# Channel mix of a two-layer sequence model: two halves of 128 channels summed on GpSimd ahead of one averaging product, and another order of squares and scaling

## The reference

```python
def _layernorm(x, g, b):
    m = jnp.mean(x, axis=-1, keepdims=True)
    v = jnp.mean(jnp.square(x - m), axis=-1, keepdims=True)
    return (x - m) * jax.lax.rsqrt(v + LN_EPS) * g + b
...
xp = jnp.concatenate([x[:, -1:], x[:, :-1]], axis=1)
xn = _layernorm(x, g2, b2)
kk = xn @ W_cm                                  # 256 -> 1024
kk = kk * cmk4 + xp4 * (1.0 - cmk4)
rr = jax.nn.sigmoid(xn * cmr + xp * (1.0 - cmr))
vv = jnp.square(jax.nn.relu(kk)) @ W_cp         # 1024 -> 256
x = x + rr * vv
```

## Time and profile before

| | us |
|---|---|
| median of 3 timed runs | 2118.95 (2117.96 to 2119.46) |
| the profiled execution's own time | 2109.22 |
| span of the profiled execution | 2107.5 |
| channel mix, from the block's start to the next stage's first product | some 1205 to 1436 |
| PE busy over the span | 1907.0 (90%) |
| DVE busy | 1357.6 (64%) |
| ACT busy | 963.3 (46%) |
| POOL busy | 247.8 (12%) |

### The profile page before, as it was taken

One profiled execution on the slowest core, in us unless ns is written; L12 is line 12 of the kernel. 1 busy time (PEld: TensorE's weight loads), 2 busy tenths in 40 slices (PEclk: granted clock), 3 DMA queues, 4 the chain that ended last, 5 costly groups with the idle time before them and its releaser, 6 DMA issues. The chain is left out here.

```text
span 2107.5 us, 31872 instructions
## 1 busy us (share of the span) xinstructions
PE 1907.0 (90%) x11154; PEld 1617.0 (77%) x11154; DVE 1357.6 (64%) x2810; ACT 963.3 (46%) x1801; POOL 247.8 (12%) x229
## 2 busy tenths in 40 slices
PE   8999999983999999996777589998999999999999
PEld 5788888872899999994445357776888888888887
DVE  7567788774666666665999878884444445345342
ACT  4656666643444444435888555542323232232221
POOL 0000012334233232331000000000000000000000
PEclk9999999995999999998888789999999999999999
DMA  3299411323544332233223413413000000000000
GB/s 105 72 364 408 149 49 59 113 84 106 144 106 88 81 85 47 41 46 110 70 60 90 97 44 120 160 51 139 1 21 20 0 20 9 11 20 0 20 11 11
DMA packets 86146, 170.32 MB, mean 81 GB/s; under 512 B 7264, under 2 KB 49888, under 8 KB 85856
## 3 DMA queue, kind: packets, MB, share of 16 engines
q1 hardware_dynamic: 65968, 132.47, 18.0%
q0 software_dynamic: 18176, 33.70, 8.1%
q10 hardware_dynamic: 1888, 2.67, 0.4%
HBM read 91.61 MB, written 88.74 MB: 86 GB/s over the span
## 5 line engine op out<-in xcount | busy, mean ns | idle before, releaser
L2690 ACT ACTIVATE x_tok<-bank,scl 128x512 f32<-128x512 f32 x128 | 88.3, 690 | 360.2 <-PE bank L2741 359.4
L2740 PE MATMUL bank<-hAh,ffn_h 128*128 128x512 f32 x512 | 202.7, 396 | 0.7 <-DVE x_tok L2617 0.7
L2740 PE MATMUL bank<-hBh,ffn_h 128*128 128x512 f32 x512 | 201.7, 394 | 0.0
L2741 PE MATMUL bank<-hAl,ffn_h 128*128 128x512 f32 x512 | 199.4, 389 | 0.0
L2741 PE MATMUL bank<-hBl,ffn_h 128*128 128x512 f32 x512 | 199.3, 389 | 0.0
L1487 POOL DMA_INDIRECT tokens_behind_spare_rows<-yg,row_of_token x70 | 129.5, 1850 | 302.7 <-DVE row_of_token L1655 283.1
L1590 ACT ACTIVATE h<-bank,b1s 128x256 f32<-128x256 f32 x280 | 124.8, 472 | 31.9 <-PE bank L1415 19.8
L2598 DVE CAST hBh<-x_tok 128x1024 fp32r<-128x1024 f32 x48 | 33.3, 693 | 157.6 <-ACT x_tok L2690 157.0
L2598 DVE CAST hAh<-x_tok 128x1024 fp32r<-128x1024 f32 x48 | 33.3, 693 | 148.7 <-ACT x_tok L2690 148.2
L911 ACT ACTIVATE L<-bank 128x512 f32<-128x512 f32 x128 | 75.4, 595 | 106.1 <-PE bank L1169 105.9
L1177 PE MATMUL bank<-st,L 128*128 128x128 f32 x768 | 116.3, 278 | 6.3 <-DVE st L549 6.2
(11 more groups left out here) (447 smaller groups left out, 5498.6 us busy)
## 6 DMA issues: line engine op xcount, KB each, us to landing
z_by_expert<-zero SPq DMA_DIRECT2D x64, 520.0 KB, 16.0
ckb<-in_ffn_dram POOLq DMA_DIRECT2D x32, 352.0 KB, 3.5
xg<-z_by_expert SPq DMA_DIRECT2D x36, 260.0 KB, 3.3
x_tok<-in_w_dram SPq DMA_DIRECT2D x8, 1024.0 KB, 7.7
ffn_h<-ffn_copy SPq DMA_DIRECT2D x2, 4096.0 KB, 14.9
x_tok<-after_time_mix SPq DMA_DIRECT2D x15, 512.0 KB, 7.5
st<-in_w_dram SPq DMA_DIRECT2D x6, 1024.0 KB, 7.3
x_tok<-x_T SPq DMA_DIRECT2D x9, 512.0 KB, 4.2
```

The source lines that it names most:

```text
L2690: A_.activation(gq[:, m % 4, :], B[2 + m % 4][:, :], ACT.Gelu, scale=scl[:, off[nm] + m:off[nm] + m + 1]).then_inc(g_act, 1)
L2740: T.matmul(out, w, x[0], start=first, stop=False)
L2741: return T.matmul(out, w, x[1], start=False, stop=last)
```

## The change

On POOL, a new section adds the two halves: `hm` = half 0 + half 1 of the block ahead of its mean, and `hv` = the same of the squares. PE then runs one product of `avg` with the sum, in place of two. `hm` lies in the place of `rs`, so POOL's sum for block b waits until scale(b-1) has read `rs` (`xs_rdy`), until mean(b-1) has read `hm` (`mean_ps`), and for the block's load. `hv` waits for the squares and for variance(b-1). On ACT, squares(b+1) now comes ahead of parts(b+1), which moves behind deviation(b+1). On DVE, scale(b+1) moves from behind low(b, 1) to ahead of square_keys(b, 2).

```diff
+        hm, hv = rs, in_x_tok(1536, BT)
+        hm_rdy, hv_rdy = sem("mean_halves_summed"), sem("square_halves_summed")
...
+        @block.gpsimd
+        def _(pool):
+            P = nc.gpsimd
+
+            def sum_mean(b):
+                pool.wait_ge(cin_ld[b % 2], loaded(b))
+                pool.wait_ge(xs_rdy, b)
+                pool.wait_ge(mean_ps, b)
+                P.tensor_tensor(hm[:, :], IN[:, b % 2, 0, 0, :], IN[:, b % 2, 0, 1, :], ALU.add).then_inc(hm_rdy, 1)
+
+            def sum_squares(b):
+                pool.wait_ge(sqr_rdy, b + 1)
+                pool.wait_ge(var_ps, b)
+                P.tensor_tensor(hv[:, :], sq[:, 0, :], sq[:, 1, :], ALU.add).then_inc(hv_rdy, 1)
+
+            for b in range(1, NB + 1):
+                sum_mean(b)
+                sum_squares(b)
...
                     keys(b, i)
                     if i == PAIRS - 1 and nxt:
                         low_x(b + 1)
+                    if i == PAIRS - 2:
+                        scale(b + 1)
                     square_keys(b, i)
                     low(b, i - 1)
-                    if i == PAIRS - 2:
-                        scale(b + 1)
...
                 high(b, 0)
-                if nxt:
-                    parts(b + 1)
                 squares(b + 1)
                 high(b, 1)
                 deviation(b + 1)
+                if nxt:
+                    parts(b + 1)
                 high(b, 2)
...
             def mean(b):
-                pe.wait_ge(cin_ld[b % 2], loaded(b))
-                for k in range(KT):
-                    last = nc.tensor.matmul(B[0][:, :], avg[:, :], IN[:, b % 2, 0, k, :], start=(k == 0), stop=(k == KT - 1))
-                last.then_inc(mean_ps, 1)
+                pe.wait_ge(hm_rdy, b)
+                nc.tensor.matmul(B[0][:, :], avg[:, :], hm[:, :], start=True, stop=True).then_inc(mean_ps, 1)
 
             def variance(b):
-                pe.wait_ge(sqr_rdy, b + 1)
-                for k in range(KT):
-                    last = nc.tensor.matmul(B[1][:, :], avg[:, :], sq[:, k, :], start=(k == 0), stop=(k == KT - 1))
-                last.then_inc(var_ps, 1)
+                pe.wait_ge(hv_rdy, b)
+                nc.tensor.matmul(B[1][:, :], avg[:, :], hv[:, :], start=True, stop=True).then_inc(var_ps, 1)
```

## The result

The changed kernel takes 2109.22 us, median of 6 runs (2107.51 to 2113.44), against 2118.45 (2116.54 to 2119.46). The ratio is 0.9960, with a 95% interval of 0.9947 to 0.9972: faster by some 8.5 us, between 6 and 11 (the two medians differ by 9.2). The forecast was 2112.3.

A forecast was written before the change was run, and what follows sets the result against it. A 26.3 us loop through DVE's values, PE's products and variance, then DVE and ACT, not the mean, bounds the kernel. Iterations 0 to 7 sum to -6.65 us: median 2118.95 becomes 2112.3; range -4 to -9.5 us.

The forecast's parts named there:

- The loop runs past the mean: In iterations 2 to 7 the 0.86 us saved on the mean buys nothing, since PE still waits for DVE's values.
- The variance saves 0.86: On PE the variance lies on the loop; one product fewer saves 0.86 us per iteration if hv is in time.
- POOL first by 0.18 us, the square held to 2.2 us: POOL's sum of squares starts 0.18 us ahead of DVE's square_keys(b, 1), which then takes 2.2 in place of 1.22 us.
- The order gives 0.07, the hold costs 0.2: Scale's new place on DVE gains 0.07 us; POOL's hold of square_keys delays Exp, so scale waits 0.2 us.
- Steady iterations -0.7 each: Iterations 2, 3, 4, 6 and 7: 0.86 + 0.07 - 0.2, about 0.7 us saved each, together -3.5.
- Iteration 5, a late mean for 0.85: A late load makes POOL's sum and the mean late, costing 0.85 us against 0.7 gained: +0.15.
- rival (3): Bubbles of 1 us at the mean bring PE's clock down, 2.5 us in each of six iterations: 2127; chance 5%.
- Iteration 0: Squares move forward and the variance starts 0.9 us earlier, at PE's low clock: -1.5 us, bounds 0.8 and 2.8.
- Iteration 1: No values to wait for, so mean and variance both count, 1.71 us, and 0.07 for the order: -1.8.
- Rival 1: DVE's square_keys starts ahead of POOL, so hv comes 1.2 us late: 2119.8, no change; chance 0.26.
- Rival 2: POOL gets no turn between DVE instructions that follow each other; PE stands 2.4 us: 2128.2; chance 0.16.
- rival 4: A float32 product of a sum on PE takes as long as two, so nothing is saved: 2121; chance 3%.

The follow-up runs named there:

- mean alone: The changed kernel with the variance back to two products and both old orders, only the mean's halves summed on POOL; ratio 1.0000 to the unchanged kernel.
- after: The kernel with the full change, against the unchanged kernel; 2109.22 us, ratio 0.9960.
- orders alone: Only the two new orders on ACT and DVE, no POOL sums, two products each; ratio 0.9981 to the unchanged kernel.
- parts ahead: The changed kernel with ACT's old order, parts back ahead of squares; ratio 1.0033 to the unchanged kernel.
- POOL second: The changed kernel, but POOL's sum of squares also waits until DVE has ended square_keys(b, 1); ratio 1.0051 to the unchanged kernel.

## Why the prediction was right, point by point

- *The loop runs past the mean.* Right. The mean alone gave a ratio of 1.000, and PE's 0.85 us of new waiting equals what was saved. A count of passes (32 fewer at 0.43 us, 13.7 us) would have promised twice the gain. The passes did fall by 32, and PE's busy time in the stage by 12.0 us (211.7 to 199.6), for 6.85 us of time. I had looked for some 13 us in PE's busy time over the whole execution, and there it fell by 7.3 only (1907.0 to 1899.7), as other stages, in which no line differs, moved by some us the other way.
- *The variance saves 0.86.* The step was right; the size is 0.95: from its start to the second half of keys(b, 2) it is 3.82 us against 4.72, and the 36 products before it took 0.05 less.
- *POOL's sum, 1.29 us.* It is 1.26 to 1.30 where nothing holds it.
- *POOL first by 0.18 us, the square held to 2.2 us.* Right to the hundredth, because both starts hang on the same DVE run: POOL's by way of centre and squares, the square's by way of centre and keys.
- *The Trainium skill's rule* (SBUF — State Buffer, Who interferes with whom) holds here for two SBUF inputs, which rows 9 could not show: the square and low are held for the rest of POOL's instruction, and POOL for the rest of theirs. Keys, with one SBUF input and one in PSUM, kept their 0.75 us beside POOL's sum.
- *The order gives 0.07, the hold costs 0.2.* The first was mis-sized: it is 0.31, with a hold of 0.25. The net on the way to L was put at a loss of 0.13 and came out as a gain of 0.06. Parts' cover held: high(b, 2) starts 0.03 us behind the end of the square that it needs.
- *Steady iterations -0.7 each.* They gave -0.87 to -0.99 (a pitch of 25.3, where I had put 25.6), by the points on the variance and the order: some 1.3 us more than forecast over five.
- *Iteration 5, a late mean for 0.85.* Mechanism right, size wrong: iteration 5 is 2.77 over its neighbours in after, of which 0.39 was there before. In the sum it stood at +0.15, and it measured +1.41: an error of 1.3, the other way. The load landed 0.9 us later against L than I had put it, and behind 2.45 us of idle the clock fell. I had named the fall as a rival (3) for six iterations at once; of iterations 2 to 7 it came in this one alone.
- *Iteration 0.* -0.88 for -1.5, within its bounds. The variance starts 3.70 us behind centre's start in place of 4.62, the 0.9 that I had put, and the way to L is 0.3 shorter. The two passes saved, 1.9 us at the low clock, came back as 0.15: from the variance to the second half of keys(0, 2) it is 6.47 us against 6.62, since the products behind ran at the low clock, 0.43 us apart, until 1230.6. And centre itself came 0.5 us later behind the stage's start. POOL's sum is a loss in this iteration: with the orders alone the variance starts 2.36 us behind centre's start, and the iteration gains 2.44.
- *Iteration 1.* -2.61 for -1.8. Some 0.25 of the difference is the order's; the rest was not traced.
- *The rivals.* Rival 1 did not come, by the 0.18 us. Rival 2's ground is gone by the rows of iteration 1, and rival 4's by the 32 passes. Rival 1's sum has a slip: iteration 5 stands in it at 1.5, where its own terms, 0.27 and 0.85, give 1.1.

That the total is so near is in part luck, as the errors cancel (+0.6, -0.8, -1.3 and +1.3 us): 6.65 forecast, 6.85 in the profiles, 8.5 (6 to 11) in the runs.

## What to carry to other kernels

Busy time names the engine, not the loop. Write one iteration down as start times on every engine, and ask of each saved microsecond which wait ends next; here, in the steady iterations, one of two equal savings counted in full and the other not at all until three other steps had been moved. When work goes to POOL beside a busy DVE, place its start against DVE's two-input instructions to a tenth of a microsecond, and look at which loads have to be there before it. Look also at what has little to spare: a late load that had cost 0.4 us cost 2.8. And change one thing at a time: two moved steps alone gave 4.2 of the 6.85 us.

## What the runs showed of the hardware that I had not expected

- Between POOL's and DVE's instructions that exclude each other, POOL got its turn after one, though DVE ran without a gap (2.15 us for its own 1.28). It loses a whole turn when it starts just after a DVE instruction: 0.06 us behind one, its sum took 2.28 us (parts ahead).
- Two ACT instructions with no open wait between them start 0.97 us apart although the first takes 1.06, and a DVE step that waits for nothing of the one before follows it by 0.67 where one that does follows by 0.78. On the way to L these made up most of the 0.24 us between the 6.89 forecast and the 6.65 measured.
- PE's granted clock fell to 0.50 behind 2.45 us of idle (after, iteration 5), was 0.66 over 5 us behind 2.13 (POOL second, iteration 2), and stayed at 1.00 behind 2.09 (the same kernel, iteration 3) and behind 1.74 (mean alone, iteration 5).
- In iteration 0, behind 6.77 us of idle PE, half the variance's passes were saved and only 0.15 of 1.9 us came back, as the low clock lasted over more of the products behind.
